# The second layer's aggregation: every block split into high and low halves, some of the low halves made by GpSimd

## The chip, the cores and the metric

The kernel runs on one core of one Trainium2 chip. The metric is the device time of one execution in microseconds (us). Three runs of the kernel before gave 1409.19, 1409.19 and 1410.59 us, a median of 1409.19 us.

## The reference, cut to what matters

Two layers follow each other. Each one adds to x (5000 nodes, 128 features) first a graph step, then a mixture-of-experts network. The graph step of the second layer multiplies the 5000 x 5000 adjacency by the normalised features:

```python
x = x + _L0_gnn_ref(_layernorm(x), adj, L0_gnn_h0, L0_gnn_y)
x = x + _L0_ffn_ref(_layernorm(x)[None], ...)[0]
x = x + _L1_gnn_ref(_layernorm(x), adj, adj, L1_gnn_weight, L1_gnn_bias)
x = x + _L1_ffn_ref(_layernorm(x)[None], ...)[0]

def _L1_gnn_ref(node_features, edge_features, adj, weight, bias):
    neighbor_node_features = adj @ node_features
    neighbor_edge_features = jnp.einsum('ij,ji->i', adj, edge_features)[:, None]
    support = jnp.concatenate((node_features, neighbor_node_features, neighbor_edge_features), axis=1)
    return support @ weight + bias
```

The change touches the product `adj @ node_features` of this step alone. Behind the graph step a router picks two of eight experts for each node.

## The kernel before, in words

**Tiling.** Nodes are padded to 5120: 40 blocks of 128 rows (NB) and 10 chunks of 512 columns (CH, CW); the last chunk is 392 columns wide. The second layer's loop is `z_iteration(k, agg, mid)`, written once for each engine and run for k = 0 to 10. In iteration k the aggregate of chunk k is summed over the 40 blocks in one PSUM bank (banks u and agg by turns, `z_bank`), while the middle part for chunk k-1 runs between the blocks: bias, edge term, product with the weights, residual add, normalisation statistics, transposes, router, ranks, row weights, and the scatter of the chunk's rows to memory. Each engine walks through 43 steps s; the table `Z_AT` (L121) says at which step a piece of the middle part stands, and within a step the order of the statements is the order of the engine's queue. TensorE uses block b at step b + 2; ScalarE, VectorE and GpSimd work on block s at step s. Engines meet only through semaphores.

**Blocks.** `plain(k, b)` (L130) decides how a block is multiplied. A plain block is one float32 matmul, L963, straight from the adjacency ring; the trace shows it as two MATMUL records. All blocks of chunk 0 and every fourth block (b % 4 == 3) of the later chunks are plain. The other 30 blocks of a chunk are split: ScalarE casts the block to fp32r, the high half (L1220), VectorE subtracts it from the block, the low half (L1766, by the helper `split_low`, L398 in the profile), and TensorE does three fp32r matmuls, high features by high half, high by low, low features by high half (L968 to L970). High and low halves lie in a ring of five buffers (`ADJ_BUFS`, `adj_part`): four over the tile wb, one over m. ScalarE's cast of a block waits until TensorE is through with the split block five before it.

**Loads.** SP loads four blocks at a time (1024 KB, `z_load`, L639) into a ring of five slots, each once TensorE is through with the four blocks that lay there.

**The other work of the engines in this loop.** VectorE, in the order of its queue: the bias add (step 1, L1774), the edge update (step 2, L1782, four instructions), the residual add (step 11, L1791, which waits for TensorE's product of step 10, L984 and L986), statistics and variance (steps 12 and 13), the normalisation (step 16, L1279), the router's logits, top-two, ranks and places (steps 21 to 31), the row weights (step 33, L1346 to L1361). ScalarE: copies out of PSUM. GpSimd: the power -1/2 of the variance (step 14, L1859), which waits for VectorE's variance and on which the normalisation waits, and at step 36 eight indirect DMAs that scatter the chunk's rows (L1873), on which the next chunk's normalisation waits.

In the first layer's loop VectorE multiplies a PSUM bank with the adjacency (L1635), and GpSimd takes the same power.

Of the kernel before, what the change touches and what calls it, by code (L numbers as in the profile page):

```python
# [20 lines left out]
NB = CH * CW // P  # L21
# [6 lines left out]
LB = 4  # L28
# [98 lines left out]
          "top": (13, 14, 15), "exp": 13, "weights": 19, "rank": 17, "place": 19, "scatter": 21}  # L127


def plain(k, b):  # L130

    return k == 0 or b % 4 == 3


SPLITS = NB - NB // 4


def split_at(b):
    return b // 4 * 3 + b % 4


def split_block(i):
    return i // 3 * 4 + i % 3


def width(k):
# [9 lines left out]
def bass_two_layer_gnn_moe_kernel(nc, x_t, adj_in, adj_out, h0_t, y_t, wr0, w1s, b1_0, w2s, b2_0,  # L156
# [17 lines left out]
    def sem(name):  # L174
        return ctx.enter_context(nc.semaphore(name))
# [136 lines left out]
    y_dram = [nc.dram_tensor(f"y_scratch{i}", [2 * P * NB, D], F32, kind="Internal").ap() for i in range(2)]  # L312

    consts_set = sem("consts_set")
    ident_zeroed, every_set, nulls_set = sem("ident_zeroed"), sem("every_set"), sem("nulls_set")
    picks_zeroed = sem("picks_zeroed")
    x_landed = [sem(f"x_landed{i}") for i in range(4)]
    weights_landed = sem("weights_landed")
    up_landed = sem("up_landed")
# [34 lines left out]
    back_shift = sem("back_shift")  # L354
    back_chain, back_var, back_rstd = sem("back_chain"), sem("back_var"), sem("back_rstd")
    back_made, back_high, back_low = sem("back_made"), sem("back_high"), sem("back_low")
    adj_high, adj_low = sem("adj_high"), sem("adj_low")
    aux_made, aux_turned, auxf_made = sem("aux_made"), sem("aux_turned"), sem("auxf_made")
    y_landed = [sem(f"y_landed{i}") for i in range(CH)]
    sum_chain, out_made, out_written = sem("sum_chain"), sem("out_made"), sem("out_written")  # L360
# [6 lines left out]
    def wait(eng, s, value):  # L367

        if isinstance(value, int) and value <= 0:
            return  # L370
        eng.wait_ge(s, value)
# [317 lines left out]
    def _(pe):  # L689
# [258 lines left out]
        def z_iteration(k, agg, mid):  # L948
            S, n, at = SZ, width(k), Z_LAST if k == CH else Z_AT
            for s in range(STEPS):  # L950
                if agg and LAG <= s < NB + LAG:
                    b = s - LAG
                    if b == 0:
                        wait(pe, S["aggf_made"], k - 1)
                    if k == 0 and b % TB == 0:
                        pe.wait_ge(back_made, b // TB + 1)
                    if k == 1 and b == 0:
                        pe.wait_ge(back_low, CH)
                        pe.wait_ge(back_high, CH)
                    if plain(k, b):  # L960
                        l = b // LB
                        wait(pe, ring_landed[l % 5], z_landed(k, l))
                        pe.matmul(z_bank(k)[:, 0:n], xn[:, b, :], slot_part(l % 5, b % LB, n),  # L963
                                  start=b == 0, stop=b == NB - 1).then_inc(S["agg_blocks"], 1)
                    else:
                        wait(pe, adj_low, (k - 1) * SPLITS + split_at(b) + 1)
                        hi, lo = adj_part(0, b)[:, 0:n], adj_part(1, b)[:, 0:n]
                        pe.matmul(z_bank(k)[:, 0:n], xnh[:, b, :], hi, start=b == 0, stop=False)  # L968
                        pe.matmul(z_bank(k)[:, 0:n], xnh[:, b, :], lo, start=False, stop=False)  # L969
                        pe.matmul(z_bank(k)[:, 0:n], xnl_rows[:, b, :], hi, start=False, stop=b == NB - 1  # L970
                                  ).then_inc(S["agg_blocks"], 1)
                if mid and s == at["turn_aux"]:
                    j = k - 1
                    wait(pe, posn_read, CH + j)
                    wait(pe, aux_made, j + 1)
                    transposes(lambda t: aux[:, t, :], aux_turned)
                if mid and s == at["product"]:
                    j = k - 1
                    wait(pe, auxf_made, j + 1)
                    wait(pe, S["aggf_made"], j + 1)  # L980
                    if k == 1:
                        pe.wait_ge(graph_weights_landed, 48)
                    for t in range(TB):
                        pe.matmul(misc[:, t * P:(t + 1) * P], auxf[:, t * P:(t + 1) * P], wgs[:, 0, :],  # L984
                                  start=True, stop=False)
                        last = pe.matmul(misc[:, t * P:(t + 1) * P], aggf[:, t * P:(t + 1) * P], wgs[:, 1, :],  # L986
                                         start=False, stop=True)
                    last.then_inc(S["agg_turned"], 1)
                if mid and s == at["turn"]:
                    turn_norm(S, k - 1)  # L990
                if mid and s == at["router"]:
                    router(S, k - 1, 1)
                if mid and s == at["rank"]:
                    count_ranks(k - 1 + CH)
                if k == CH - 1 and s == STEPS - 1:
                    turn_in(TILES)
                if k == CH:
                    tile_beside(1, s)
# [258 lines left out]
    def _(dve):  # L1257
# [489 lines left out]
        def z_iteration(k, agg, mid):  # L1747
            S, at = SZ, Z_LAST if k == CH else Z_AT
            for s in range(STEPS):
                if k == 0:  # L1750
# [7 lines left out]
                        back_split(s // TB - 2)  # L1758
                    if s == STEPS - 1:
                        back_split(CH - 1)  # L1760
                if agg and s < NB and not plain(k, s):
                    l = s // LB
                    if s % LB == 0:
                        wait(dve, ring_landed[l % 5], z_landed(k, l))
                    wait(dve, adj_high, (k - 1) * SPLITS + split_at(s) + 1)
                    split_low(dve, adj_part(1, s)[:, 0:width(k)], slot_part(l % 5, s % LB, width(k)),  # L1766
                              adj_part(0, s)[:, 0:width(k)]).then_inc(adj_low, 1)
# [57 lines left out]
    def _(pool):  # L1825
        pool.memset(mhalf[:], -0.5)
        pool.memset(euler[:], float(np.e))
        pool.memset(picks[:], 0.0).then_inc(picks_zeroed, 1)
        pool.wait_ge(picks_zeroed, 1)
        pool.memset(picks[:, 31:32], 1.0)  # L1830
        pool.iota(prio[:], [[0, TB], [-1, E]], base=E, channel_multiplier=0, allow_small_or_imprecise_dtypes=True)
        pool.memset(ident[:], 0.0).then_inc(ident_zeroed, 1)
        pool.wait_ge(ident_zeroed, 1)
        pool.affine_select(out=ident[:], in_=ident[:], compare_op=ALU.not_equal, fill=1.0, base=0,
                           pattern=[[-1, P]], channel_multiplier=1).then_inc(consts_set, 1)

# [4 lines left out]

        input_power(0)
        pool.memset(yo[:], 0.0).then_inc(nulls_set, 1)
        pool.memset(every[:], 1.0).then_inc(every_set, 1)
        pool.wait_ge(every_set, 1)
        pool.affine_select(out=upper[:], in_=every[:], compare_op=ALU.is_gt, fill=0.0, base=0,
                           pattern=[[1, P]], channel_multiplier=-1)
        pool.iota(base[:], [[REGION, E]], base=0, channel_multiplier=0, allow_small_or_imprecise_dtypes=True)
# [62 lines left out]
        def z_iteration(k, agg, mid):  # L1911
            at = Z_LAST if k == CH else Z_AT
            for s in range(STEPS):
                if k == 0 and s % TB == 0 and s // TB < CH:
                    power(s, back_var, back_rstd, s // TB + 1)
                if mid and s == at["power"]:
                    power(0, SZ["mid_var"], SZ["mid_rstd"], k)
                if mid and s == at["scatter"]:
                    for i in range(2 * TB):
                        scatter_rows(1, CH + k - 1, i)  # L1920
                if k == CH and s in (8, 10, 14, 18):
                    scatter_tile(TILES + (8, 10, 14, 18).index(s))
# [68 lines left out]
```

## Time and profile before

| | us |
|---|---|
| median of 3 runs | 1409.19 |
| profiled execution, span | 1406.8 |
| TensorE busy | 1294.1 |
| VectorE busy | 922.4 |
| ScalarE busy | 645.5 |
| GpSimd busy | 426.3 |
| second layer's loop, chunks 1 to 9, about | 926 to 1237 |

The profiled execution's own time is its span; nothing else of it was recorded, and it is 2.4 us under the median. PE is TensorE's matmuls, PEld its weight loads, DVE VectorE, ACT ScalarE, POOL GpSimd, SP the engine that issues loads. Matmuls overlap in the records, so the time of one is read from the starts of neighbours; the same holds for VectorE's and ScalarE's instructions in a row, whose records overlap by less than 0.1 us.

### The profile page before, as it was taken

The page shows a single profiled execution, that of the slowest core. Times are in us where ns is not written, and L with a number is a line of the kernel's source. Part 1 is how long each engine was busy: PE and PEld are TensorE (multiplying, and loading weights), DVE is VectorE, ACT ScalarE, POOL GpSimd, SP SyncE. Part 2 cuts the span into 40 slices and gives each one's busy share as a digit, 9 for nine tenths or more (in the row PEclk, how much of TensorE's full clock was granted, in tenths as well). Part 3 has the DMA queues.
Part 4 walks back from the last instruction along what each step waited for, and adds up shares of the span by engine and source line. Part 5 has one row for each costly group of instructions (what it writes and reads, how often), then busy time and mean ns, then how long its engine had stood idle before and what let it go on. Part 6 is the DMA issues. An engine that isn't in the chain of part 4 may idle for free.

```text
span 1406.8 us, 20911 instructions
## 1 busy us (share of the span) xinstructions
PE 1294.1 (92%) x6560; PEld 818.7 (58%) x6560; DVE 922.4 (66%) x2683; ACT 645.5 (46%) x1175; POOL 426.3 (30%) x427
## 2 busy tenths in 40 slices
PE   5899999999999999999989999999998999988950
PEld 2344445454545454554778998466666666766840
DVE  7776877777686877777542232877776777854323
ACT  3445444443434444343444554665555555543420
POOL 2102020202020202021365554302322333267772
PEclk9999999999999999999999999999999999999985
DMA  9798998889898979798559993789897988846846
GB/s 311 244 355 296 363 352 333 284 318 318 288 347 269 361 252 357 252 335 267 203 175 406 334 303 117 287 291 314 316 317 270 323 316 311 271 124 181 246 135 226
DMA packets 120974, 399.76 MB, mean 284 GB/s; under 512 B 19920, under 2 KB 51170, under 8 KB 91552
## 3 DMA queue, kind: packets, MB, share of 16 engines
q1 hardware_dynamic: 80512, 339.66, 69.1%
q10 hardware_dynamic: 28288, 34.98, 7.1%
q0 software_dynamic: 12064, 23.80, 4.6%
q8 instruction: 52, 0.85, 0.2%
q14 instruction: 58, 0.48, 0.1%
HBM read 346.44 MB, written 56.89 MB: 287 GB/s over the span
## 4 chain that ended last, share of the span: by engine, by line
PE 26%; DVE 11%; issue 8%; POOL 5%; DMA 2%; ACT 2%; POOLq 0%; SPq 0%; DVEq 0%; ACTq 0%
PE d L896 6%; POOL y_scratch L1882 3%; DVE adj_over_wb L398 3%; PE u L963 2%; PE agg L963 2%; PE u L880 2%; PE agg L968 1%; POOL rows_scratch L1873 1%; PE u L968 1%; PE agg L970 1%; PE agg L969 1%; PE u L970 1%; PE u L969 1%; PE u L882 1%; PE u L881 1%
## 5 line engine op out<-in xcount | busy, mean ns | idle before, releaser
L787 PE MATMUL agg<-m,xn 128*128 128x512 f32 (+1 forms) x800 | 402.8, 586 | 0.0
L1117 ACT ACTIVATE mabs<-m 128x512 f32<-128x512 f32 (+1 forms) x400 | 239.7, 617 | 309.4 <-DVE m L1635 208.6
L1635 DVE TENSOR_TENSOR m<-s,ring 128x512 f32<-128x512 f32 (+1 forms) x400 | 268.8, 675 | 149.0 <-PE s L763 128.1
L763 PE MATMUL s<-ymov,ysta 128*128 128x512 f32 (+1 forms) x400 | 263.3, 659 | 24.8 <-DVE m L1635 15.8
L1873 POOL DMA_INDIRECT rows_scratch<-xrow,idx x160 | 170.1, 1063 | 295.6 <-DVE xrow L1361 104.0
L787 PEld LDWEIGHTS agg<-m,xn 128*128 128x128 f32 x800 | 151.9, 190 | 68.5 <-issue 48.1
L1882 POOL DMA_INDIRECT y_scratch<-yo,ids x144 | 142.2, 987 | 83.5 <-issue 52.0
L763 PEld LDWEIGHTS s<-ymov,ysta 128*128 128x128 f32 x400 | 76.0, 190 | 153.7 <-issue 95.2
L398 DVE TENSOR_TENSOR adj_over_wb<-ring,adj_over_wb 128x512 fp32r<-128x512 f32 (+1 forms) x216 | 138.9, 673 | 34.5 <-ACT adj_over_wb L1220 32.1
L1220 ACT CAST adj_over_wb<-ring 128x512 fp32r<-128x512 f32 (+1 forms) x216 | 125.8, 607 | 52.4 <-PE agg L970 26.3
L1859 POOL TENSOR_TENSOR rstd<-vareps,mhalf 128x4 f32<-128x4 f32 x30 | 38.6, 1286 | 365.7 <-DVE vareps L1273 365.7
L837 PE MATMUL d<-mabs,picks 128*32 128x512 f32 (+1 forms) x800 | 99.1, 595 | 0.0
L1645 DVE CUSTOM_DVE_ANT_0 ring<-ring 128x512 f32<-128x512 f32 (+1 forms) x132 | 88.2, 670 | 2.8 <-DMA ring<-in_adj_out 2.7
L1154 ACT ACTIVATE h<-u,wb 128x256 f32<-128x256 f32 (+1 forms) x96 | 53.2, 554 | 77.3 <-PE u L882 77.2
L963 PE MATMUL u<-ring,xn 128*128 128x512 f32 x160 | 77.3, 598 | 2.5 <-ACT xn L1197 2.4
L1500 DVE TENSOR_TENSOR tile_x<-s,tile_x 128x512 fp32r<-128x512 f32 x24 | 16.6, 691 | 94.5 <-ACT tile_x L1146 94.5
L896 PE MATMUL d<-wb,h 128*128 128x128 f32 x528 | 73.3, 276 | 0.0
L896 PEld LDWEIGHTS d<-wb,h 128*128 128x128 f32 x528 | 67.9, 193 | 1.7
L968 PE MATMUL agg<-adj_over_wb,ysta 128*128 128x512 f32 (+1 forms) x120 | 62.7, 522 | 4.6 <-DVE adj_over_wb L398 3.8
L837 PEld LDWEIGHTS d<-mabs,picks 128*32 128x32 f32 x800 | 19.4, 109 | 68.4 <-issue 53.3
L1645 DVE CUSTOM_DVE_ANT_0 stage<-ring,stage 128x512 f32<-128x512 f32 (+1 forms) x88 | 58.2, 663 | 0.0
L1901 POOL TENSOR_TENSOR ex<-euler,top 128x4 f32<-128x4 f32 x10 | 10.3, 1028 | 146.1 <-DVE top L1324 129.0
(278 smaller groups left out, 2270.3 us busy)
## 6 DMA issues: line engine op xcount, KB each, us to landing
ring<-in_adj_in SPq DMA_DIRECT2D x180, 1024.0 KB, 6.0
ring<-in_adj_out SPq DMA_DIRECT2D x30, 1024.0 KB, 7.8
rows_scratch<-yo ACTq DMA_DIRECT2D x81, 260.0 KB, 7.2
wb<-blob_scratch SPq DMA_DIRECT2D x24, 834.0 KB
stage<-in_adj_out SPq DMA_DIRECT2D x19, 1024.0 KB, 9.4
ring<-in_adj_in SPq DMA_DIRECT2D x20, 784.0 KB, 5.2
wb_more<-blob_scratch SPq DMA_DIRECT2D x15, 834.0 KB
xt<-rows_scratch SPq DMA_DIRECT2D x60, 130.0 KB, 4.1
```

The lines of the kernel that those rows point to most:

```text
L398: return eng.tensor_tensor(low, raw, high.bitcast(F32), ALU.subtract)
L763: pe.matmul(sbank[s % 2][:, 0:width(k)], ysta[:, s * P:(s + 1) * P], ymov[:, k % 2, 0:width(k)], start=True, stop=True).then_inc(s_made, 1)
L787: pe.matmul(abank[:, 0:n], xn[:, b, :], m[:, b % M_BUFS, 0:n], start=b == 0, stop=b == NB - 1).then_inc(S["agg_blocks"], 1)
L837: last = pe.matmul(dbank[1][32 * i:32 * i + 32, 0:width(k)], pick[0], mabs[:, (g * GROUPS + i) % ABS_BUFS, 0:width(k)], start=g == 0, stop ...
L896: last = pe.matmul(dbank[t % 2][:, q * D:(q + 1) * D], h[:, n % H_BUFS, q * P:(q + 1) * P], tile_part(t, "down", hb, q * parts_of(t) // TB ...
L963: pe.matmul(z_bank(k)[:, 0:n], xn[:, b, :], slot_part(l % 5, b % LB, n), start=b == 0, stop=b == NB - 1).then_inc(S["agg_blocks"], 1)
L1117: act.activation(mabs[:, b % ABS_BUFS, 0:width(k)], m[:, b % M_BUFS, 0:width(k)], ACT.Abs).then_inc(abs_made, 1)
L1220: act.copy(adj_part(0, s)[:, 0:width(k)], slot_part(l % 5, s % LB, width(k))).then_inc(adj_high, 1)
L1635: dve.tensor_tensor(m[:, s % M_BUFS, 0:width(k)], sbank[s % 2][:, 0:width(k)], slot_part(LOAD_AT[k, l, False][0], s % LB, width(k)), ALU.m ...
L1645: dve.tensor_tensor_reduce(part, slot_part(into, b % LB, width(k)), part, 1.0, 0.0, ALU.mult, ALU.add, rpart[:, k, b:b + 1]).then_inc(edge ...
L1873: pool.indirect_dma_start(out=rows_dram, out_offset=bass.IndirectOffsetOnAxis(ap=idx[:, t, c:c + 1], axis=0), in_=xrow[:, t, c, :], in_off ...
L1882: pool.indirect_dma_start(out=y_dram[layer], out_offset=bass.IndirectOffsetOnAxis(ap=ids[:, buf, q:q + 1], axis=0), in_=yo_part(t)[:, q, : ...
```

## The change

From chunk 1 on no block is plain: all 40 blocks of a chunk are split. The low halves of five blocks per chunk (b = 15, 19, 23, 27, 31) are made by GpSimd with the same subtraction, the other 35 by VectorE, and TensorE waits on a semaphore of its own for GpSimd's (`adj_low_pool`). The ring of five buffers now turns over with every block. On GpSimd the low half of block s stands at step s, ahead of the other work of that step. Three semaphores of the constants are merged into one, `consts_chain`, with the waits kept.

```diff
+def by_pool(b):
+    return b % 4 == 3 and 15 <= b < 35
+
 def plain(k, b):
-    return k == 0 or b % 4 == 3
+    return k == 0
 
-SPLITS = NB - NB // 4
+SPLIT_BLOCKS = [b for b in range(NB) if not plain(1, b)]
+SPLITS = len(SPLIT_BLOCKS)
+POOL_SPLITS = sum(by_pool(b) for b in SPLIT_BLOCKS)
 
 def split_at(b):
-    return b // 4 * 3 + b % 4
+    return SPLIT_BLOCKS.index(b)
 
 def split_block(i):
-    return i // 3 * 4 + i % 3
+    return SPLIT_BLOCKS[i]
+
+def low_count(k, b):
+    before = [c for c in SPLIT_BLOCKS[:split_at(b) + 1] if by_pool(c) == by_pool(b)]
+    return (k - 1) * (POOL_SPLITS if by_pool(b) else SPLITS - POOL_SPLITS) + len(before)
...
-    adj_high, adj_low = sem("adj_high"), sem("adj_low")
+    adj_high, adj_low, adj_low_pool = sem("adj_high"), sem("adj_low"), sem("adj_low_pool")
...
-                        wait(pe, adj_low, (k - 1) * SPLITS + split_at(b) + 1)
+                        wait(pe, adj_low_pool if by_pool(b) else adj_low, low_count(k, b))
...
-                if agg and s < NB and not plain(k, s):
+                if agg and s < NB and not plain(k, s) and not by_pool(s):
...
+                if agg and s < NB and by_pool(s) and not plain(k, s):
+                    l = s // LB
+                    wait(pool, ring_landed[l % 5], z_landed(k, l))
+                    wait(pool, adj_high, (k - 1) * SPLITS + split_at(s) + 1)
+                    split_low(pool, adj_part(1, s)[:, 0:width(k)], slot_part(l % 5, s % LB, width(k)),
+                              adj_part(0, s)[:, 0:width(k)]).then_inc(adj_low_pool, 1)
                 if mid and s == at["power"]:
                     power(0, SZ["mid_var"], SZ["mid_rstd"], k)
```

## Rows read from the trace of the kernel before

**Rows 1.** The page, part 1: busy time, share, instructions of each engine.

```profile
PE 1294.1 (92%) x6560; PEld 818.7 (58%) x6560; DVE 922.4 (66%) x2683; ACT 645.5 (46%) x1175; POOL 426.3 (30%) x427
```

**Rows 2.** Busy by stretch: length, PE, PEld, DVE, ACT, POOL, PEclk, DMA share, GB/s.

```profile
1137.00:1172.00 35.00, 34.28 (x152) 24.00 (x151) 27.54 (x79) 20.00 (x38) 10.90 (x10) 1.00 0.89 317
```

**Rows 3.** Waits, 917 to 1241 us: who waited for whom: total, times, longest.

```profile
DVE adj_over_wb L398 <- ACT adj_over_wb L1220: 32.1, 19, 2.3
...
PEld agg L968 <- DVE adj_over_wb L398: 16.4, 33, 1.1
...
DVE xrow L1279 <- DMA rows_scratch<-xrow,idx: 5.4, 4, 3.9
```

**Rows 4.** Timeline, VectorE: start, us, engine, line, operation, tiles, [idle before <-releaser].

```profile
232.16 0.69 DVE L1635 TENSOR_TENSOR m<-s,ring 128x512 f32<-128x512 f32 x1 [0.67 <-PE s L763]
...
884.67 0.69 DVE L398 TENSOR_TENSOR xnl<-xn,ysta 128x512 fp32r<-128x512 f32 x1
...
965.35 0.69 DVE L1791 TENSOR_TENSOR xres<-xres,misc 128x512 f32<-128x512 f32 x1 [2.28 <-PE misc L986]
...
1025.86 1.13 DVE L1782 SCALAR_TENSOR_TENSOR xres<-m,redge,xres 128x128 f32<-128x128 f32 x4
...
1035.42 0.69 DVE L1791 TENSOR_TENSOR xres<-xres,misc 128x512 f32<-128x512 f32 x1 [2.28 <-PE misc L986]
...
1043.94 1.29 DVE L398 TENSOR_TENSOR adj_over_wb<-ring,adj_over_wb 128x512 fp32r<-128x512 f32 x2 [1.41 <-ACT adj_over_wb L1220]
...
1049.06 0.69 DVE L398 TENSOR_TENSOR adj_over_wb<-ring,adj_over_wb 128x512 fp32r<-128x512 f32 x1
...
1054.87 0.24 DVE L1346 COPY xrow<-tokid 128x4 f32<-128x4 f32 x2
...
1056.04 1.92 DVE L398 TENSOR_TENSOR adj_over_wb<-ring,adj_over_wb 128x512 fp32r<-128x512 f32 x3
...
1059.69 0.68 DVE L1774 TENSOR_TENSOR xres<-xres,m 128x512 f32<-128x512 f32 x1
```

**Rows 5.** Timeline, TensorE's matmuls, 1033 to 1057 us.

```profile
1033.36 0.38 PE L984 MATMUL misc<-m 128*128 128x128 f32 x2
...
1035.07 0.48 PE L968 MATMUL u<-adj_over_wb,ysta 128*128 128x512 f32 x1
...
1040.02 1.02 PE L963 MATMUL u<-ring,xn 128*128 128x512 f32 x2
...
1041.11 0.40 PE L969 MATMUL u<-adj_over_wb,ysta 128*128 128x512 f32 x1
...
1055.12 0.40 PE L970 MATMUL u<-adj_over_m,xnl 128*128 128x512 f32 x1
...
1055.82 0.40 PE L970 MATMUL u<-adj_over_wb,xnl 128*128 128x512 f32 x1
1056.78 0.50 PE L968 MATMUL u<-adj_over_wb,ysta 128*128 128x512 f32 x1 [0.56 <-DVE adj_over_wb L398]
```

**Rows 6.** Timeline, ScalarE's casts.

```profile
1043.21 1.66 ACT L1220 CAST adj_over_wb<-ring 128x512 fp32r<-128x512 f32 x3
...
1055.56 0.62 ACT L1220 CAST adj_over_m<-ring 128x512 fp32r<-128x512 f32 x1 [0.94 <-PE u L970]
```

**Rows 7.** Timeline, GpSimd: the power in the first and second layer.

```profile
231.57 1.04 POOL L1859 TENSOR_TENSOR rstd<-vareps,mhalf 128x4 f32<-128x4 f32 x1 [27.51 <-DVE vareps L1273]
...
884.77 1.45 POOL L1859 TENSOR_TENSOR rstd<-vareps,mhalf 128x4 f32<-128x4 f32 x1 [1.69 <-DVE vareps L1273]
...
1038.66 1.41 POOL L1859 TENSOR_TENSOR rstd<-vareps,mhalf 128x4 f32<-128x4 f32 x1 [5.69 <-DVE vareps L1273]
```

**Rows 8.** Groups by line and shape, GpSimd: busy us, mean ns of one, idle before.

```profile
L1843 POOL MEMSET yo<- 128x1024 f32 x1 | 0.9, 941 | 0.0
...
L1834 POOL TENSOR_SCALAR_AFFINE_SELECT ident<-ident 128x128 f32<-128x128 f32 x1 | 0.3, 292 | 0.2 <-POOL ident L1832 0.2
...
L1832 POOL MEMSET ident<- 128x128 f32 x1 | 0.2, 195 | 0.0
```

More of the change, by code:

```diff
@@ L314, in bass_two_layer_gnn_moe_kernel @@
     consts_set = sem("consts_set")
-    ident_zeroed, every_set, nulls_set = sem("ident_zeroed"), sem("every_set"), sem("nulls_set")
-    picks_zeroed = sem("picks_zeroed")
+    consts_chain, nulls_set = sem("consts_chain"), sem("nulls_set")
     x_landed = [sem(f"x_landed{i}") for i in range(4)]
@@ L1827, in _ @@
         pool.memset(euler[:], float(np.e))
-        pool.memset(picks[:], 0.0).then_inc(picks_zeroed, 1)
-        pool.wait_ge(picks_zeroed, 1)
+        pool.memset(picks[:], 0.0).then_inc(consts_chain, 1)
+        pool.wait_ge(consts_chain, 1)
         pool.memset(picks[:, 31:32], 1.0)
         pool.iota(prio[:], [[0, TB], [-1, E]], base=E, channel_multiplier=0, allow_small_or_imprecise_dtypes=True)
-        pool.memset(ident[:], 0.0).then_inc(ident_zeroed, 1)
-        pool.wait_ge(ident_zeroed, 1)
+        pool.memset(ident[:], 0.0).then_inc(consts_chain, 1)
+        pool.wait_ge(consts_chain, 2)
         pool.affine_select(out=ident[:], in_=ident[:], compare_op=ALU.not_equal, fill=1.0, base=0,
@@ L1843, in _ @@
         pool.memset(yo[:], 0.0).then_inc(nulls_set, 1)
-        pool.memset(every[:], 1.0).then_inc(every_set, 1)
-        pool.wait_ge(every_set, 1)
+        pool.memset(every[:], 1.0).then_inc(consts_chain, 1)
+        pool.wait_ge(consts_chain, 3)
         pool.affine_select(out=upper[:], in_=every[:], compare_op=ALU.is_gt, fill=0.0, base=0,
```

## The prediction, made before the result was known

> **What bounds the kernel now.** The page comes first: TensorE is busy 92% of the span of 1406.8 us and VectorE 66% [rows 1]. A share says nothing of a stage, so next I asked for busy time by stretch: in one chunk of the second layer's loop (35 us) TensorE is busy 34.3, VectorE 27.5, ScalarE 20.0, GpSimd 10.9 us, at full granted clock (1.00, the 2.4 GHz level), with the DMA engines at 0.89 [rows 2]. TensorE looks like the limit. The waits, though, show its weight loads waiting for VectorE's low halves, 33 times for one of the two banks alone, and VectorE in its turn waiting for ScalarE's casts [rows 3], which wait for TensorE [rows 6]: two engines lead by turns. Two starts of the residual add, two chunks apart, give a chunk of (1035.42 - 965.35) / 2 = 35.03 us [rows 4].
>
> The timelines show who leads where. TensorE: from L970 at 1055.12 to L970 at 1055.82, one split block of three passes takes 0.70 us, 0.23 a pass; a plain block runs from 1040.02 until its successor's first pass (whose second, L969, starts at 1041.11, so 0.23 earlier), 0.86 us [rows 5]. A chunk without stalls is 30 x 0.70 + 10 x 0.86 = 29.6, plus the small products between blocks, some 3.5 (the product at step 10 alone takes 1.7, from 1033.36 to 1035.07): 33.1 us. So about 1.9 us of each chunk are stalls. VectorE: a low half takes 0.605 us (two in a row 1.29, the last of them 0.69, so 0.60 from start to start). From low half 20 at 1043.94 until the bias add at 1059.69 it works almost without a gap: 17 low halves (10.3) and 5.45 of router work, 15.75 us [rows 4]. In the second half of a chunk VectorE is already the pacer; in the first half it idles, 2.28 us ahead of the residual add and 1.41 us ahead of low half 20 [rows 4].
>
> **The change, part by part.** Per chunk; there are nine (k = 1 to 9, the last 392 columns wide instead of 512).
>
> (a) *Ten plain blocks become split.* TensorE: 10 x (0.70 - 0.86) = -1.6 us. ScalarE gets ten more casts; three in a row take 1.66 us, the last of them 0.62 [rows 6], so 10 x 0.52 = 5.2 us on 20.0 busy of 35 [rows 2]; its idle time covers that, and without that cover its own chunk would be some 25 us, still under TensorE's. SP's queue issues the same loads on the same counts. Merging the constants' semaphores keeps every wait: nothing.
>
> (b) *The ring of five split buffers gets shorter.* Five buffers plus the plain blocks between them held some 4.9 us of TensorE's work; now 5 x 0.70 = 3.5. The way round is 2.4: own passes 0.70, last pass to cast 0.21 (1055.12 plus a pass of 0.23, to 1055.56), cast to low half 0.73 (1043.21 to 1043.94), low half to matmul 0.74 (1056.04 to 1056.78) [rows 4 to 6]; so VectorE may be away for 1.1 us, not 2.5. Its pieces of other work are that long: the edge update 1.13 with its tail, the weights 1.17 (1054.87 to 1056.04) [rows 4]. Block 3, now split, stands right behind the edge update, and blocks 34 and 35 behind the weights.
>
> (c) *Low halves 3, 7, 11, 35, 39 on VectorE*, 5 x 0.605 = 3.0 us. Those of 3, 7, 11 fall in the first half, where the 2.28 us ahead of the residual add take their 1.8. Those of 35 and 39 fall in the saturated stretch: 15.75 + 1.2 = 16.95 us. TensorE needs only 21 x 0.70 + 1.0 (router, rank) = 15.7 there, so it gains less than (a) says.
>
> (d) *Low half 15 stands behind the power in GpSimd's queue* (step 14, then 15). In the trace the power runs from 1038.66 to 1040.07, and TensorE comes to block 15 at 1040.02 [rows 5, 7]. With T for the low half, 0.05 between these two, 0.1 for a semaphore and 0.15 us for a TensorE that comes earlier by block 11's saving, block 15 waits T + 0.3. T is not in the trace: a memset of 1024 columns takes 0.94 us, so 512 columns at least 0.52; the affine select, which also reads its operand, takes 0.292 at 128 columns against 0.195 for a memset of that size, 0.76 ns more per column, so two reads and the write make 512 x (0.83 + 1.52) ns + 0.1 us = 1.3 [rows 8]. I take the middle, T = 0.9: wait 1.2. By the Trainium skill (GPSIMD Engine Reference, section 3.1), a two-input operation costs about 2.6 cycles per element at 1.2 GHz, an estimated 1.11 us; by it the sum below would be some 7 us higher.
>
> Parts (a) to (d) make these stalls, each the time at which VectorE (or GpSimd) has the block ready, less the time at which TensorE wants it:
> - Block 3: VectorE ends low half 1 as TensorE starts the chunk; bias 0.6, low half 2 0.6, edge 1.05, low half 3 to matmul 0.74 make 3.0; TensorE is there after 3 x 0.70 = 2.1: 0.9.
> - Blocks 13 and 14, counted from the product's end: 0.35 to the residual add (1035.07 to 1035.42 [rows 4, 5]), 0.6 for it, 0.6 for low half 12, some 0.8 for the statistics, 0.74: 13 is ready at 3.1, wanted at 2.8: 0.3. Low half 13 and the variance's 0.5 put 14 at 4.2, wanted at 3.8: 0.4.
> - Block 15: 1.2, from (d).
> - Block 26: low half 20 starts about 0.3 ahead of block 19. From it to low half 26 VectorE takes 5.1 (1043.94 to 1049.06 [rows 4]), with 0.74 and less 0.3 5.6; TensorE wants 26 after 7 x 0.70 = 4.9: 0.7.
> - Block 34: from low half 26 to 34 VectorE takes 7.0 (1049.06 to 1056.04 [rows 4]), 0.2 of it a wait; TensorE's eight blocks and the ranks take 5.9: 0.9.
>
> Together 4.4, on a stall-free chunk of 40 x 0.70 + 3.5 = 31.5: 35.9, against 35.0 now: **+0.9**.
>
> (e) *GpSimd and VectorE at the same operands' door.* The power takes 1.45 us where VectorE is just subtracting two SBUF tiles (at 884.77, beside the xnl low half at 884.67 [rows 4]), and 1.04 in the first layer, where VectorE has nothing under way as it starts (at 231.57; the next instruction is at 232.16) [rows 4, 7]. So GpSimd's read waits for a VectorE instruction with two SBUF inputs. The power reads four columns; that VectorE waits in turn for a long GpSimd read isn't shown. Bounds per low half: 0, and T. I take T, because a low half on GpSimd reads for most of its time and the rows show the two excluding each other. Low half 15 falls beside the normalisation (one tile in) and 19 into VectorE's wait for ScalarE's casts; 23, 27 and 31 fall into the saturated stretch: 3 x 0.9 = 2.7, of which 0.6 goes into waits already counted: **+2.1**. The Trainium skill states it both ways (SBUF — State Buffer, section "Who interferes with whom"): a VectorE instruction with two SBUF inputs and a GpSimd one that reads SBUF shut each other out for a whole instruction. The trace agrees for the GpSimd side (1.45 against 1.04 us), and shows nothing of the other.
>
> GpSimd's scatters (step 36) follow low half 31 in its queue but start on VectorE's weights as now; the next normalisation, which needs them landed, waits for them 4 times in the whole loop, 5.4 us in all [rows 3], and itself comes no sooner than now: nothing.
>
> **Sum.** 0.9 + 2.1 = 3.0 per full chunk; 8 x 3.0 + 0.77 x 3.0 = 26 us. The profiled execution spans 1406.8, 2.4 below the median of 1409.2; I put the difference on the median: **1435 us**. Ends of the unknowns: T = 0.52 gives 1.0 for (e) and 0.8 for (d), together 1.5 per chunk, 1422; T = 1.3 gives 3.3 and 1.6, together 4.6, 1449.
>
> **Rivals.**
> 1. *No exclusion for VectorE*: (e) is 0, 0.9 per chunk, 8 us: 1417. For: the rows show GpSimd waiting, not VectorE. Against: the power there reads four columns and would hold VectorE for a moment at most, so they could not show it.
> 2. *Faster: TensorE's saving arrives.* Its place is block 15 and the stretch behind it: if GpSimd's low half takes about 0.5 us and doesn't hold VectorE, block 15 waits 0.8, VectorE has five blocks' rest in the stretch where it is short (TensorE's 4 x 0.70 against 3 x 0.605 per group) and the stalls shrink to some 2.5: 31.5 + 2.5 = 34.0, -1.0 per chunk, 1400. It decides where the stalls of a chunk stay under 3.5 us. For: TensorE's 1.6 us are certain. Against: VectorE's 30.6 us of work per chunk (35 x 0.605 and, from 27.5 busy less 30 x 0.605, 9.4 of other work) beside TensorE's 31.5 leaves no room for its forced waits.
> 3. *A wash*: stalls grow by just the 1.6 us saved: within 2.8 us of 1409. It is the crossing between 1 and 2.
>
> **How the numbers follow.** Exclusion as in (e): 0.60, 1422 to 1449. Rival 1: 0.15, 1413 to 1421. Rival 2: 0.17, 1394 to 1406. Rival 3: 0.08. A measurement of this kernel tells 0.2% (2.8 us) from no change. Faster 0.17, same 0.08, slower 0.75. From 1403 to 1448 leaves out the better part of rival 2 and a few in a hundred above; the likeliest case's own range is 1422 to 1449.
>
> **What would show it.** GpSimd's subtractions of 0.5 to 1.3 us (longer where they wait); VectorE's low halves beside them at 1.3 us and more instead of 0.69, at blocks 20 to 34; TensorE waiting at block 15 for GpSimd by about 1.2 us in each chunk; residual adds some 38 us apart instead of 35.0. I am wrong if the low halves beside GpSimd's keep 0.69, or if the residual adds come closer together than 35.0.

## The result, and the profile after

The changed kernel is **slower: 1450.87 us** (median of four runs, 1448.97 to 1452.91) against 1409.19 for the kernel before; the ratio is 1.0291, interval 1.0254 to 1.0328. Forecast were 1435 us and a range up to 1448: the direction is right, the loss is 41.7 us instead of 26, and the time lies above the range.

In the code after, the lines named so far stand 12 further down: the low half is L410 (on VectorE and on GpSimd alike), a split block's three passes L980 to L982, ScalarE's cast L1232, the normalisation L1291, the residual add L1803, the power L1871, the scatter L1885. The page, part 1, of the changed kernel [rows 1]:

```profile
span 1451.2 us, 21316 instructions
...
PE 1293.5 (89%) x6650; PEld 829.5 (57%) x6650; DVE 986.0 (68%) x2728; ACT 699.9 (48%) x1265; POOL 510.6 (35%) x472
```

TensorE's sum is unchanged, VectorE's is 63.6 us longer, though it makes only five low halves more per chunk (9 x 3.0 = 27 us). The rest is in how long its instructions last. The residual adds of the second layer's loop, VectorE's timeline after [rows 4]:

```profile
930.85 0.69 DVE L1803 TENSOR_TENSOR xres<-xres,misc 128x512 f32<-128x512 f32 x1 [1.51 <-PE misc L998]
...
1051.03 0.69 DVE L1803 TENSOR_TENSOR xres<-xres,misc 128x512 f32<-128x512 f32 x1 [1.49 <-PE misc L998]
...
1091.06 0.69 DVE L1803 TENSOR_TENSOR xres<-xres,misc 128x512 f32<-128x512 f32 x1 [1.51 <-PE misc L998]
...
1285.74 0.69 DVE L1803 TENSOR_TENSOR xres<-xres,misc 128x512 f32<-128x512 f32 x1 [6.70 <-PE misc L998]
```

A chunk takes 40.03 us, where 35.03 stood before and 38 was forecast. From the first add to the last it is 1285.74 - 930.85 = 354.9 us against 313.2 (930.32 to 1243.55): 41.7 us more. The two profiled spans differ by 44.4 us (1451.2 - 1406.8), so all but 2.7 us of that lies in this stretch. One of those chunks by the view of busy time (columns as in [rows 2]):

```profile
1051.03:1091.06 40.03, 34.52 (x162) 25.24 (x161) 35.45 (x84) 26.17 (x46) 16.08 (x14) 1.00 0.82 277
```

TensorE is as busy as before in five more us of chunk; VectorE went from 27.54 to 35.45. Five low halves at 0.605 explain 3.0 of these 7.9; 4.9 us are instructions that last longer than they should. The timelines say which. GpSimd in that chunk (the power, then low halves 15, 19, 23, 27, 31):

```profile
1054.28 1.41 POOL L1871 TENSOR_TENSOR rstd<-vareps,mhalf 128x4 f32<-128x4 f32 x1 [1.13 <-DVE vareps L1285]
1055.68 1.25 POOL L410 TENSOR_TENSOR adj_over_wb<-ring,adj_over_wb 128x512 fp32r<-128x512 f32 x1
1056.90 1.28 POOL L410 TENSOR_TENSOR adj_over_m<-ring,adj_over_m 128x512 fp32r<-128x512 f32 x1
1062.86 1.29 POOL L410 TENSOR_TENSOR adj_over_wb<-ring,adj_over_wb 128x512 fp32r<-128x512 f32 x1 [4.67 <-ACT adj_over_wb L1232]
1066.67 1.38 POOL L410 TENSOR_TENSOR adj_over_wb<-ring,adj_over_wb 128x512 fp32r<-128x512 f32 x1 [2.52 <-ACT adj_over_wb L1232]
1070.86 1.40 POOL L410 TENSOR_TENSOR adj_over_wb<-ring,adj_over_wb 128x512 fp32r<-128x512 f32 x1 [2.81 <-ACT adj_over_wb L1232]
```

VectorE in the same chunk:

```profile
1055.83 2.95 DVE L1291 TENSOR_SCALAR xrow<-xres,mv,rstd 128x128 f32<-128x128 f32 x4 [0.44 <-POOL rstd L1871]
...
1062.91 1.28 DVE L1313 TENSOR_TENSOR lg<-lg,red 128x32 f32<-128x32 f32 x1
...
1067.03 1.07 DVE L1338 TENSOR_TENSOR rank<-lg,top 128x32 f32<-128x32 f32 x1
...
1071.02 1.79 DVE L410 TENSOR_TENSOR adj_over_wb<-ring,adj_over_wb 128x512 fp32r<-128x512 f32 x1
```

Lay the two side by side. Each of these four rows starts 0.05 to 0.36 us behind the start of a GpSimd low half. The two router operations last until it is over, the low half 0.55 us and the normalisation 0.60 us longer: the small router operation at 1062.91 takes 1.28 us instead of 0.19, the one at 1067.03 1.07 instead of 0.19, the low half at 1071.02 1.79 instead of 0.69, and the normalisation at 1055.83, which runs beside two of them, 2.95 instead of 1.12. Normalisation and router operations of the kernel before, in its VectorE timeline:

```profile
1040.21 1.12 DVE L1279 TENSOR_SCALAR xrow<-xres,mv,rstd 128x128 f32<-128x128 f32 x4 [0.44 <-POOL rstd L1859]
...
1045.59 0.19 DVE L1301 TENSOR_TENSOR lg<-lg,red 128x32 f32<-128x32 f32 x1
...
1048.61 0.19 DVE L1326 TENSOR_TENSOR rank<-lg,top 128x32 f32<-128x32 f32 x1
```

Held: 1.09 + 0.88 + 1.10 + 1.83 = **4.9 us**, the missing sum.

Not every operation is held. A reduction with one operand in this chunk, and the normalisation two chunks earlier, in VectorE's timeline after:

```profile
1066.82 0.18 DVE L1336 TENSOR_REDUCE top<-lg 128x4 f32<-128x32 f32 x1
...
977.49 1.27 DVE L1291 TENSOR_SCALAR xrow<-xres,mv,rstd 128x128 f32<-128x128 f32 x4 [2.38 <-DMA rows_scratch<-xrow,idx]
```

The reduction runs wholly inside the GpSimd low half of 1066.67 and takes its usual 0.18 us. The normalisation at 977.49 had waited 2.38 us for the scatters, came behind low half 15 and was held by 0.15 only, yet its chunk takes 40.34 us. In the regular chunks of the full width the normalisation is over 7.7 to 8.0 us behind the residual add, by the hold or by the wait, and 5.9 us in the kernel before (1040.21 + 1.12 - 1035.42).

What TensorE makes of it, its matmuls' waits in that chunk [rows 5]:

```profile
1056.99 0.50 PE L980 MATMUL u<-adj_over_wb,ysta 128*128 128x512 f32 x1 [1.19 <-POOL adj_over_wb L410]
...
1064.85 0.50 PE L980 MATMUL u<-adj_over_wb,ysta 128*128 128x512 f32 x1 [0.77 <-DVE adj_over_wb L410]
...
1069.10 0.50 PE L980 MATMUL u<-adj_over_wb,ysta 128*128 128x512 f32 x1 [1.10 <-DVE adj_over_wb L410]
...
1072.86 0.50 PE L980 MATMUL u<-adj_over_wb,ysta 128*128 128x512 f32 x1 [0.40 <-DVE adj_over_wb L410]
...
1077.17 0.50 PE L980 MATMUL u<-adj_over_m,ysta 128*128 128x512 f32 x1 [0.71 <-DVE adj_over_m L410]
```

The first is block 15, waiting for GpSimd; the others wait for VectorE, each a little behind one of the held instructions or, the last, behind the weights.

### The profile page after: what moved, and what is told of

Same layout as the page of the kernel before. It is cut to its first block, busy times and chain, and to the rows that moved or that the text cites. A ratio compares the mean times of both kernels' runs of the same rounds, so it can differ in the third digit from the quotient of the medians.

```text
span 1451.2 us, 21316 instructions
## 1 busy us (share of the span) xinstructions
PE 1293.5 (89%) x6650; PEld 829.5 (57%) x6650; DVE 986.0 (68%) x2728; ACT 699.9 (48%) x1265; POOL 510.6 (35%) x472
## 4 chain that ended last, share of the span: by engine, by line
DVE 15%; PE 13%; POOL 11%; issue 11%; DMA 4%; ACT 2%; POOLq 0%; SPq 0%; DVEq 0%
POOL rows_scratch L1885 7%; PE d L908 6%; DVE adj_over_wb L410 3%; POOL y_scratch L1894 3%; DMA rows_scratch<-xrow,idx 2%; PE u L892 2%; DVE xrow L1291 1%; PE u L894 1%; PE u L893 1%; DVE xres L1740 1%; PE u L887 1%; PE s L871 1%; DVE adj_over_m L410 1%; DVE lg L1313 1%; DVE xres L1832 1%
## 5 line engine op out<-in xcount | busy, mean ns | idle before, releaser
L1885 POOL DMA_INDIRECT rows_scratch<-xrow,idx x160 | 194.1, 1213 | 185.4 <-DVE idx L1391 89.7
L1232 ACT CAST adj_over_wb<-ring 128x512 fp32r<-128x512 f32 (+1 forms) x288 | 166.7, 609 | 46.2 <-PE agg L982 20.9
L410 DVE TENSOR_TENSOR adj_over_wb<-ring,adj_over_wb 128x512 fp32r<-128x512 f32 (+1 forms) x252 | 171.2, 709 | 18.9 <-ACT adj_over_wb L1232 16.5
L1871 POOL TENSOR_TENSOR rstd<-vareps,mhalf 128x4 f32<-128x4 f32 x30 | 38.3, 1277 | 344.2 <-DVE vareps L1285 344.2
L980 PE MATMUL agg<-adj_over_wb,ysta 128*128 128x512 f32 (+1 forms) x160 | 67.4, 421 | 22.2 <-DVE adj_over_wb L410 16.2
L410 POOL TENSOR_TENSOR adj_over_wb<-ring,adj_over_wb 128x512 fp32r<-128x512 f32 (+1 forms) x36 | 46.9, 1302 | 91.2 <-ACT adj_over_wb L1232 91.2
L980 PE MATMUL u<-adj_over_wb,ysta 128*128 128x512 f32 x128 | 54.5, 426 | 17.9 <-DVE adj_over_wb L410 12.8
L982 PE MATMUL agg<-adj_over_wb,xnl 128*128 128x512 f32 (+1 forms) x160 | 61.6, 385 | 0.0
```

What stands on the lines that cost most here:

```text
L410: return eng.tensor_tensor(low, raw, high.bitcast(F32), ALU.subtract)
L1232: act.copy(adj_part(0, s)[:, 0:width(k)], slot_part(l % 5, s % LB, width(k))).then_inc(adj_high, 1)
L1885: pool.indirect_dma_start(out=rows_dram, out_offset=bass.IndirectOffsetOnAxis(ap=idx[:, t, c:c + 1], axis=0), in_=xrow[:, t, c, :], in_off ...
```

## The experiments

All chunk times below are distances of residual adds in the profiled run, without the irregular chunk told of at the end and the two shorter ones at the end of the loop. The runs of the kernel before beside them had medians of 1411.29 (numbers 1, 2, 5 and 6), 1415.39 (3, 7, 8 and 9) and 1411.05 us (4 and 10).

**1. All forty low halves on VectorE.**

```diff
 def by_pool(b):
-    return b % 4 == 3 and 15 <= b < 35
+    return False
```

> All 40 blocks split, all 40 low halves on VectorE, none on GpSimd. Exclusion (GpSimd's reads hold VectorE): VectorE has 40 x 0.605 + 9.4 = 33.6 us of work per chunk plus about 2 us of forced waits, 35.6 to 37: 1415 to 1427 us, well below the 1450.9 of the change although VectorE does more. Ring and load alone (GpSimd innocent): VectorE carries 3.0 us more per chunk than in the change, so 1451 to 1477 us.

Measured: 1430.81 us, ratio 1.0142 (1.0114 to 1.0169); 36.9 us in the two chunks where the normalisation waits for nothing, 37.4 to 38.6 in four others, where it waits 0.2 to 1.3 us for the scatters. One of each, VectorE's timeline (residual adds at 968.11 and 1006.72):

```profile
974.39 1.11 DVE L1291 TENSOR_SCALAR xrow<-xres,mv,rstd 128x128 f32<-128x128 f32 x4 [1.33 <-DMA rows_scratch<-xrow,idx]
...
1011.59 1.11 DVE L1291 TENSOR_SCALAR xrow<-xres,mv,rstd 128x128 f32<-128x128 f32 x4
```

It is over 7.4 us behind the residual add in the first, in a chunk of 38.6, and 6.0 us in the second, in one of 36.9: about as much as the normalisation comes later, the chunk is longer. The time is above the 1415 to 1427 expected of exclusion, and far below the other theory's 1451. VectorE has 3.0 us more to do per chunk than in the change, and the chunk is 1.4 to 3.1 us shorter. Normalisation, the two router operations and all low halves have their old durations (1.11, 0.19, 0.19 and 0.69). So GpSimd's help costs more than the work that it takes over. The other part of the loss stands here too: without any low half on GpSimd the forty splits cost some 20 us against the kernel before.

**2. The same plan, but GpSimd only writes.** The five low halves are filled with zeros; the low part of these blocks is left out.

```diff
-                    split_low(pool, adj_part(1, s)[:, 0:width(k)], slot_part(l % 5, s % LB, width(k)),
-                              adj_part(0, s)[:, 0:width(k)]).then_inc(adj_low_pool, 1)
+                    pool.memset(adj_part(1, s)[:, 0:width(k)].bitcast(F32), 0.0).then_inc(adj_low_pool, 1)
```

> As the change, but GpSimd's five low halves per chunk are memsets to zero: same queue, same waits, same buffers, a write and no read (the low part of these blocks is left out of the sum). Exclusion through the read: VectorE's instructions beside them keep their length, GpSimd's take about 0.52 us, chunk 35 to 36 us, 1409 to 1420 us. If a GpSimd write held VectorE as well: VectorE's neighbours would show 0.5 us more each and the chunk be near 37, 1425 us. Ring and load alone: 1440 to 1450 us.

Measured: 1418.75 us, ratio 1.0053 (1.0033 to 1.0073); 35.7 to 36.1 us a chunk, one of 37.2. The groups of GpSimd by shape, then one row of GpSimd's timeline and two of VectorE's from this run:

```profile
L1932 POOL MEMSET adj_over_wb<- 128x512 f32 x32 | 16.8, 524 | 81.0 <-ACT adj_over_wb L1232 81.0
```

```profile
1049.36 0.53 POOL L1932 MEMSET adj_over_wb<- 128x512 f32 x1 [4.70 <-ACT adj_over_wb L1232]
```

```profile
1049.43 0.19 DVE L1313 TENSOR_TENSOR lg<-lg,red 128x32 f32<-128x32 f32 x1
1049.54 0.69 DVE L410 TENSOR_TENSOR adj_over_wb<-ring,adj_over_wb 128x512 fp32r<-128x512 f32 x1
```

GpSimd writes 512 columns beside the same router operation, and it keeps its 0.19 us; the low half behind it keeps its 0.69. So it is the reading that holds these, not the writing. The normalisation is the exception: it takes 1.22 to 1.42 us instead of 1.12 in five of this run's chunks, for instance here:

```profile
1007.65 1.40 DVE L1291 TENSOR_SCALAR xrow<-xres,mv,rstd 128x128 f32<-128x128 f32 x4 [0.44 <-POOL rstd L1871]
```

Memsets ran beside it from 1007.48 to 1007.99 and again from 1008.40. In all 40.0 - 35.8 = 4.2 us of each chunk hang on GpSimd's subtracting. Not all of that is the hold: the memset is also 0.7 us shorter, and TensorE waits 0.42 us for block 15 instead of 1.19. With memsets the plan stands 0.8 us above the 35.0 of before.

**3. GpSimd reads one operand instead of two** (it copies the high half; the low part of those blocks is left out).

```diff
-                    split_low(pool, adj_part(1, s)[:, 0:width(k)], slot_part(l % 5, s % LB, width(k)),
-                              adj_part(0, s)[:, 0:width(k)]).then_inc(adj_low_pool, 1)
+                    pool.tensor_copy(adj_part(1, s)[:, 0:width(k)],
+                                     adj_part(0, s)[:, 0:width(k)].bitcast(F32)).then_inc(adj_low_pool, 1)
```

> GpSimd copies the high half into the low half's buffer in place of the subtraction, for the same five blocks: it reads one operand instead of two (the low part of those blocks is left out, a second high part stands there). If any long read of SBUF by GpSimd holds VectorE's two-input operations, the neighbours are held by about one copy each (0.6 to 1.0 us) and the residual adds stand 37.0 to 39.0 us apart, 1427 to 1442 us. If only a two-input operation holds them, it is as with the memset: 35.7 to 36.0 apart, 1419 us, and VectorE's low halves beside them keep 0.69 us.

Measured: 1428.31 us, ratio 1.0083 (1.0054 to 1.0112); 36.9 us a chunk. The copies take 0.60 to 0.72 us. VectorE's timeline beside them:

```profile
1011.15 1.70 DVE L1291 TENSOR_SCALAR xrow<-xres,mv,rstd 128x128 f32<-128x128 f32 x4 [0.45 <-POOL rstd L1871]
...
1017.15 0.59 DVE L1313 TENSOR_TENSOR lg<-lg,red 128x32 f32<-128x32 f32 x1
...
1020.57 0.39 DVE L1338 TENSOR_TENSOR rank<-lg,top 128x32 f32<-128x32 f32 x1
...
1023.88 1.10 DVE L410 TENSOR_TENSOR adj_over_wb<-ring,adj_over_wb 128x512 fp32r<-128x512 f32 x1
```

The same four instructions are held, by 0.58, 0.40, 0.20 and 0.41 us: a read of one operand does it too, and by no more than its own length (the normalisation stands beside two copies). A copy is hardly longer than the memset (0.60 to 0.72 against 0.52), so the reading makes the difference, not the length. The chunk ended just below the expected 37.0.

**4. The two parts of the change's GpSimd work, one at a time.** First 23, 27 and 31 alone, then 15 and 19 alone; the others on VectorE.

```diff
-    return b % 4 == 3 and 15 <= b < 35
+    return b % 4 == 3 and 23 <= b < 35
```

> Of the change's five GpSimd low halves only 23, 27 and 31 are left; 15 and 19 go to VectorE. Measured against the version with all forty on VectorE (residual adds 36.9 us apart). Theory A, what the changed kernel's rows say: 15 and 19 hold the normalisation by 1.83 us and make TensorE wait 1.2 us at block 15, so taking them away brings most of that back: three low halves less on VectorE (-1.8) and three holds of 0.9 to 1.1 (+3.1) on 36.9 give 38.2 us, 1435 to 1441 us, and the normalisation is back at 1.1 us. Theory B, as in the prediction: 15 and 19 fall harmlessly, the loss is that of 23, 27 and 31 alone: then this is as slow as the change or slower by the 1.2 us that VectorE takes over, 39.5 us and more, 1448 us and above.

Measured: 1439.37 us, ratio 1.0192 (1.016 to 1.0223); 38.2 to 38.3 us a chunk, one of 39.4.

```diff
-    return b % 4 == 3 and 15 <= b < 35
+    return b % 4 == 3 and 15 <= b < 23
```

> The other part: GpSimd makes low halves 15 and 19 alone, VectorE 23, 27 and 31 too. Theory A: VectorE gives up 1.2 us ahead of its saturated stretch, its normalisation is held by 1.83 us and TensorE waits 1.2 us at block 15: 36.9 + 1.2 to 1.9 give 38.1 to 38.8 us, 1436 to 1446 us. Theory B: the two cost the wait at block 15 alone, less what VectorE gains: 36.5 to 37.2 us, 1424 to 1432 us.

Measured: 1440.47 us, ratio 1.0211 (1.0178 to 1.0244); 38.6 to 39.1 us a chunk. The normalisation in the two, VectorE's timeline, the first with 23, 27, 31 and the second with 15 and 19 on GpSimd:

```profile
1010.20 1.11 DVE L1291 TENSOR_SCALAR xrow<-xres,mv,rstd 128x128 f32<-128x128 f32 x4
...
1015.44 1.29 DVE L1313 TENSOR_TENSOR lg<-lg,red 128x32 f32<-128x32 f32 x1
```

```profile
1011.64 2.94 DVE L1291 TENSOR_SCALAR xrow<-xres,mv,rstd 128x128 f32<-128x128 f32 x4 [0.46 <-POOL rstd L1871]
```

Both came out in the ranges of theory A, outside those of B. On the 36.9 of the version with all on VectorE the one part costs 1.3, the other some 1.8 to 2.0 us a chunk; together 40.0 to 40.2, and the change has 40.0. From the first residual add to the last, where scatter waits and the irregular chunk count, both cost the same: 343.5 and 343.4 us against 334.6. So the two that the prediction held for harmless cost at least as much as the other three. Their share is about the delay by the hold: the normalisation is over 1.8 us later than in number 1.

**5. Low half 15 alone moved to VectorE**, so that nothing stands behind the power at block 15.

```diff
-    return b % 4 == 3 and 15 <= b < 35
+    return b % 4 == 3 and 19 <= b < 35
```

> As the change, but low half 15 on VectorE, GpSimd makes 19, 23, 27 and 31. If block 15 behind the power and the normalisation held by two GpSimd low halves in a row are 1.2 and 1.8 us of the 5 us per chunk: 1.5 to 2.2 us less per chunk, 1432 to 1438 us. If these are covered by waits that come anyway: within 4 us of 1450.9.

Measured: 1450.02 us, ratio 1.0273 (1.0249 to 1.0297): no gain over the change. The profiled run was the slowest of the five (1456.56), but from the first residual add to the last it takes 354.2 us, as the change (354.9). The typical chunk is shorter, 39.2 us, by 0.9 instead of the expected 1.5 to 2.2, and the normalisation is held once instead of twice (2.07 us at 1057.45); but behind the irregular chunk one takes 42.8 and the next 40.4. In the first of these two:

```profile
1141.86 1.11 DVE L1291 TENSOR_SCALAR xrow<-xres,mv,rstd 128x128 f32<-128x128 f32 x4 [3.00 <-DMA rows_scratch<-xrow,idx]
```

The normalisation now waits 3 us for the scatters of the chunk before, which run late (below). What the other chunks won went there and into the irregular chunk, 1.1 us longer than in the change.

**6. No GpSimd, and five plain blocks kept (15, 19, 23, 27, 31).**

```diff
 def by_pool(b):
-    return b % 4 == 3 and 15 <= b < 35
+    return False
 def plain(k, b):
-    return k == 0
+    return k == 0 or b % 4 == 3 and 15 <= b < 35
```

> Blocks 3, 7, 11, 35, 39 split with their low halves on VectorE as in the change; the five blocks that GpSimd had (15 to 31) plain as before; nothing on GpSimd. Exclusion: what is left is the load of five more low halves and a ring shorter in places: TensorE stall-free 35 x 0.70 + 5 x 0.86 + 3.5 = 32.3, stalls of 2.5 to 3.5, 1408 to 1416 us. Ring and load alone: most of the 41.7 us of the change, 1435 to 1450 us.

Measured: 1420.83 us, ratio 1.008 (1.005 to 1.011), between the two expectations and nearer the first. The first four chunks take 35.2 to 35.5 us, the later ones 37.4, where the normalisation waits up to 2.8 us for the scatters. So five more splits where VectorE has room (3, 7, 11) and where it hasn't (35, 39) come out 0.1 to 0.4 us above the kernel before at best.

**7. The ten plain blocks kept, and five of the thirty low halves on GpSimd.**

```diff
 def by_pool(b):
-    return b % 4 == 3 and 15 <= b < 35
+    return b % 4 == 2 and 18 <= b < 38
 def plain(k, b):
-    return k == 0
+    return k == 0 or b % 4 == 3
```

> The ten plain blocks of the kernel before stay plain; of its thirty low halves GpSimd makes five (18, 22, 26, 30, 34) and VectorE 25. If a GpSimd low half holds VectorE for about its own length (1.3 us, as beside block 23 in the changed kernel), VectorE gives up 5 x 0.6 = 3.0 us and is held by up to 5 x 1.3 = 6.5 us, and TensorE waits for GpSimd's results behind the casts: residual adds 36 to 38 us apart instead of 35.0, 1418 to 1435 us. If the loss of the change lay in its missing plain blocks and not in the exclusion, VectorE's relief counts: 34 to 35 us apart, 1400 to 1409 us.

Measured: 1431.91 us, ratio 1.0102 (1.0073 to 1.0131); 36.8 to 37.1 us a chunk, one of 37.6. Here VectorE is relieved of 3.0 us per chunk against the kernel before and nothing else in the plan is changed, and each chunk is some 1.9 us longer. So low halves on GpSimd lose time also where no plain block is missing. And again not all is held: the router's add of a PSUM bank and an SBUF tile (`lg<-misc,gateb`) keeps 0.18 us at 1017.03, inside a GpSimd low half of 1.36 us that begins at 1016.90.

**8. Plain at 7 instead of 15**, against number 6, for the late scatters.

```diff
-    return k == 0 or b % 4 == 3 and 15 <= b < 35
+    return k == 0 or b in (7, 19, 23, 27, 31)
```

> No low half on GpSimd; plain are 7, 19, 23, 27 and 31 (against 15, 19, 23, 27, 31 in the version with five plain blocks), so that VectorE's row of low halves 4 to 10 in the first half of a chunk is broken at 7. If the scatter instruction of 4.2 to 4.9 us is held by that unbroken row, all eight scatters stay at or under 1.5 us, the normalisation doesn't wait for them, and the residual adds stand some 35.2 to 35.6 us apart all along (block 15 adds a stall of up to 0.3 us): 1409 to 1416 us. If it is held by something else, one scatter of each chunk takes 4.2 us or more, and the chunks behind the sixth are 37.4 us again: 1418 to 1424 us.

Measured: 1417.44 us, ratio 1.0009 (0.9988 to 1.003), 35.3 to 35.8 us a chunk at first and 36.2 to 36.6 later. The long scatter is still there, 4.30 us, so the first expectation falls as it was put; the second named chunks of 37.4 us and 1418 at least, and did not come either. Why the scatter is shorter by 0.6 stands at the end.

**9. Ten plain blocks, but elsewhere.** By the timeline of before TensorE waits at blocks 26 and 34, and VectorE has rest ahead of the residual add; so 7 and 11 are split, and 26 and 34 plain. No low half on GpSimd (`by_pool` returns False, as in number 1).

```diff
 def plain(k, b):
-    return k == 0
+    return k == 0 or b in (3, 15, 19, 23, 26, 27, 31, 34, 35, 39)
```

> Still ten plain blocks and thirty splits, no low half on GpSimd: 7 and 11 become split, where VectorE waits ahead of the residual add, and 26 and 34 become plain, for which TensorE waits in the kernel before. TensorE's own work stays; if VectorE's saturated second half is what makes TensorE's 1.9 us of stalls per chunk, two low halves less there (1.2 us) take 0.5 to 1.0 us of them away: residual adds 34.0 to 34.5 us apart, 1400 to 1405 us. If the first half has no room (the ring of five buffers, or the scatters that come late), they stay 35.0 or more apart: 1409 to 1418 us.

Measured: 1405.47 us, ratio 0.9916 (0.9891 to 0.9942); 34.04 us a chunk. **Faster than both kernels**: by 0.8% than the one before, with an interval clear of 1. Eight of the nine chunks gain; the irregular one is 3.5 us longer than in the kernel before (42.38 against 38.88) and takes back a part.

**10. The same with 13 in place of 15.**

```diff
-    return k == 0 or b in (3, 15, 19, 23, 26, 27, 31, 34, 35, 39)
+    return k == 0 or b in (3, 13, 19, 23, 26, 27, 31, 34, 35, 39)
```

> From the version with plain blocks 3, 15, 19, 23, 26, 27, 31, 34, 35, 39 (34.04 us a chunk, 1405.5 us): plain block 15 becomes 13, since TensorE's largest waits left there stand at blocks 13 and 14, 0.24 and 0.32 us beyond the usual 0.24, behind the residual add and the statistics. If those are VectorE's doing, one low half less at that place takes them: 33.5 to 33.8 us a chunk, 1400 to 1404 us. If VectorE's work is only moved behind the normalisation (low half 15 now stands there), the stall turns up at block 15 or 16: 34.0 or more, 1404 to 1410 us.

Measured: 1399.0 us, ratio 0.9918 (0.9892 to 0.9944); 33.7 to 33.8 us a chunk, with two of 34.4 and 35.1, where the normalisation waits for the scatters. Busy time in one of them (columns as in [rows 2]):

```profile
964.02:997.79 33.77, 33.77 (x152) 24.20 (x151) 27.84 (x78) 20.05 (x36) 11.11 (x9) 1.00 0.89 325
```

In this view TensorE is busy all through: with VectorE's work the same as before (27.8 us), its visible stalls are gone by the choice of blocks alone. The ends of matmuls are modelled, though, and against the prediction's stall-free 33.1 us some 0.6 are left. Of numbers 9 and 10 each is measured against its own runs of the kernel before, and the intervals overlap. The typical chunk is 0.3 us shorter in 10, but the two longer ones give that back: the eight distances outside the irregular chunk sum up to 266.0 us, and to 266.4 in 9. That 10 beats 9 is not shown.

## Why the prediction was right in direction and wrong in size

**The failed step is (e), in two places.** It named the right mechanism, GpSimd's read and VectorE's two-input operations shutting each other out, and rival 1 (no exclusion) is out by numbers 1 to 3. The forecast was 38.0 us a chunk, and 40.03 came. Of the low halves that were to last 1.3 us and more beside GpSimd's, one in a chunk did; the others held are two router operations and the normalisation.

- *15 and 19 were priced at nothing, and this is most of the miss.* The prediction had 15 fall "beside the normalisation (one tile in)", an operation with a single tile from SBUF, and 19 "into VectorE's wait for ScalarE's casts". But both stand back to back behind the power, at 1055.68 and 1056.90, and the normalisation was held through both: 1.83 us. Where it came too late for them, it had waited for the scatters instead. No row of before shows the normalisation beside a long read, so it wanted a bound like every unknown cost, 0 to 2T, and got the 0 alone. The Trainium skill (SBUF — State Buffer, section "Who interferes with whom") speaks against that 0: it lists `tensor_scalar` among the operations that can take the pair of ports shared with GpSimd, in a two-port mode. The held 2.95 us agree with it; which mode the normalisation ran in no run shows.
- *T was too small.* Taken was 0.9, between the bounds 0.52 and 1.3; measured are 1.25 us back to back and up to 1.40 elsewhere. In (e) that costs little, 3.07 us held at 23, 27 and 31 instead of 2.7, because VectorE comes to the door some time behind GpSimd. The Trainium skill (GPSIMD Engine Reference, section 3.1) gave an estimated 1.11, nearer than the middle of the bounds, still short. The upper bound's assumption, that both operands pass one after the other, fits: the copy with one operand takes 0.60 us, the subtraction with two 1.25.

Put the measured holds into (e): 1.09 + 0.88 + 1.10 - 0.6 for 23, 27, 31 and 1.83 for 15 and 19 make 4.3 us instead of 2.1, and 35.03 + 0.9 + 4.3 = 40.2, where 40.03 was measured. That it comes so near is in part luck: the sum adds the wait at block 15 to the hold of the normalisation, and number 5, where that wait is gone and the hold 0.9 us shorter, gained 0.9 us a chunk and no more. Each low half of 23, 27 and 31 holds VectorE by what is left of it when VectorE comes, 0.9 to 1.1 us; (e) had put the whole T.

**Parts (a) to (d), forecast at +0.9, came out about right, one stall by luck.** With a GpSimd that only writes, the chunk is 0.8 us longer (number 2), where (d) with the memset's 0.52 would make it +0.5. Single stalls: block 15, forecast 1.2, measured 1.19; but the rule was T + 0.3, and with the measured 1.25 it would be 1.55, with the memset's 0.52 it would be 0.82, where 0.42 was measured. T was too small by 0.35 and the rest too large by as much. Blocks 13 and 14, forecast 0.3 and 0.4: their first passes start 0.93 and 1.09 us behind the block before (1052.82, 1053.75, 1054.84) instead of 0.69, so 0.24 and 0.40. Block 3, forecast 0.9, measured 0.60 (at 1044.32). Behind the weights, forecast 0.9, measured 0.71. Block 26, forecast 0.7, shows 1.10, with a held router operation in it. (a) and (b) by themselves are right in what they leave out, too: ScalarE's 26.2 busy us in a chunk of 40 leave it room; that its casts hold nobody up is not shown by a run of its own.

**The scatters were costed at nothing**, and that isn't quite so: the normalisation's waits for them rose from 5.4 to 7.7 us over the loop [rows 3]. In the change they stand in the place of the hold, and in numbers 5 and 6 they ate what the chunk had gained.

**Rival 2** (faster) put its decision at stalls under 3.5 us per chunk and a GpSimd low half of 0.5. Even the memset, which has just that length and holds only the normalisation, by up to 0.3 us, left the chunk 0.8 above before: TensorE's certain 1.6 us are used up by the waits of (a) to (d) almost alone. The runs that saved time are those that left VectorE's work as long as it was and moved it, numbers 9 and 10.

From chunk to the whole loop, 5.0 x 8.77 would be 43.9 (eight full chunks and one of 392 columns); it is 41.7, mostly because one irregular chunk of the kernel before (38.88 us) grew by 2.2 only.

## What to carry to other kernels

Before GpSimd takes work from a VectorE that is busy with operands in SBUF, count what GpSimd's reading will hold: here a subtraction worth 0.6 us on VectorE took 1.25 to 1.40 on GpSimd and held VectorE by 0.9 to 1.1 each time where a subtraction, a router operation on two SBUF tiles or the normalisation stood in its way; a reduction with one operand and an add with an operand in PSUM passed. Its writes beside VectorE held the normalisation by up to 0.3 us and the others not at all. And where two engines lead by turns, look at which blocks the stalls stand before sharing out the sum: moving two of the ten plain blocks to the stalls, with no work saved at all, took 1.0 us off every chunk of 35 but the irregular one.

## What the runs showed that was not expected

**One scatter in each of six chunks takes 4.2 to 4.9 us** in the changed kernel and in numbers 1 to 6; in the kernel before none of the loop takes over 1.5. It ends 0.83 us behind a row of VectorE's subtractions without a gap. GpSimd and VectorE in the changed kernel:

```profile
1043.81 4.90 POOL L1885 DMA_INDIRECT rows_scratch<-xrow,idx  x1 [0.30 <-issue]
```

```profile
1044.79 2.49 DVE L410 TENSOR_TENSOR adj_over_wb<-ring,adj_over_wb 128x512 fp32r<-128x512 f32 x4
1047.20 0.68 DVE L410 TENSOR_TENSOR adj_over_m<-ring,adj_over_m 128x512 fp32r<-128x512 f32 x1
```

The row ends at 1047.88, the scatter at 48.71. In number 8 the row ends at 1035.16 and the scatter at 1035.99; in number 7 at 1038.46 and 1039.29 (a scatter of 3.69 us). Same distance each time, and a row shorter by one low half makes a scatter shorter by 0.6. Yet in the kernel before a scatter at 993.66 takes 1.09 us in the midst of such a row, and numbers 9 and 10 have none over 1.5: what lets some through isn't settled, and that the row holds the scatter is not shown.

**In one chunk of every kernel GpSimd issues nothing for 5.1 to 6.5 us between two scatters**, in the kernel before from 1062.64 to 1068.51, and a chunk next to it is 0.5 to 8 us longer than its neighbours (38.88 there, 41.06 after, 42.38 in number 9). Its cause is in no view of the profile, and stays open.
